# A two-layer decoder on one core: second group of the first attention loaded in the opening stage, one context group fewer loaded ahead, maxima sent by part, two pairs summed by TensorE

## What is computed

```python
x = _layernorm(x + _L0_attn_ref(x, ...))        # 16 heads of 16, 8 masked forward, 8 backward, distance bias
x = _layernorm(x + _L0_xattn_ref(x, ctx, ...))  # 154 context keys, scores clipped at +-10000
x = _layernorm(x + _L0_ffn_ref(x, ...))         # 8 experts, top 2, gelu(x w1) * (x v1)
x = _layernorm(x + _L1_attn_ref(x, ...))        # full attention
x = _layernorm(x + _L1_xattn_ref(x, ctx, ...))  # 154 context keys
x = _layernorm(x + _L1_ffn_ref(x, ...))         # rms norm, causal attention over a latent, rms norm, 8 experts top 2
```

## Time and profile before

| what | value |
|---|---|
| median of 3 runs | 2012.9 us (2011.45 to 2017.55) |
| the profiled execution | 2015.6 us, of which the span is 2013.8 us |
| busy shares | PE 92%, DVE 65%, ACT 48%, POOL 28% |
| mean granted TensorE clock | 0.961 |
| at0, from its first matmul to t1 | about 70.7 to 318 us |
| xa0; xa1 | about 360 to 488; 1362 to 1460 us |
| t3 | about 865 to 949 us |

### The profile page before, as it was taken

One profiled execution on the slowest core, in us unless ns is written; L12 is line 12 of the kernel. 1 busy time (PEld: TensorE's weight loads), 2 busy tenths in 40 slices (PEclk: granted clock), 3 DMA queues, 4 the chain that ended last, 5 costly groups with the idle time before them and its releaser, 6 DMA issues. The chain is left out here.

```text
span 2013.8 us, 34863 instructions
## 1 busy us (share of the span) xinstructions
PE 1857.6 (92%) x12102; PEld 1066.7 (53%) x12103; DVE 1312.1 (65%) x2305; ACT 974.5 (48%) x1906; POOL 562.2 (28%) x939
## 2 busy tenths in 40 slices
PE   8799999888599999989999999987888999987997
PEld 4344445333499999955222222243344444447996
DVE  4588875798733333367988888656787888754113
ACT  3366664566121212244677777743533666632334
POOL 3212223343233333213011111133452111143551
PEclk9899999788799999999999999998998999988999
DMA  7644404410911111055412221055045244051224
GB/s 184 147 93 68 68 4 111 97 34 10 379 55 34 34 34 34 29 166 130 74 33 33 33 42 24 1 128 111 19 101 120 43 64 65 2 209 43 70 70 147
DMA packets 99099, 158.23 MB, mean 79 GB/s; under 512 B 31447, under 2 KB 79063, under 8 KB 93783
## 3 DMA queue, kind: packets, MB, share of 16 engines
q1 hardware_dynamic: 86738, 131.79, 28.7%
q0 software_dynamic: 7488, 20.46, 3.3%
q10 hardware_dynamic: 4736, 4.25, 0.6%
HBM read 110.72 MB, written 44.72 MB: 77 GB/s over the span
## 5 line engine op out<-in xcount | busy, mean ns | idle before, releaser
L2025 ACT ACTIVATE arena<-psum 128x512 f32<-128x512 f32 (+1 forms) x1120 | 575.3, 591 | 285.4 <-PE psum L1981 195.4
L1726 DVE TENSOR_REDUCE arena<-psum 128x1 f32<-128x1024 f32 (+7 forms) x384 | 427.5, 1155 | 71.1 <-PE psum L1684 46.1
L1981 PE MATMUL psum<-arena 99*128 99x512 bf16 (+7 forms) x1280 | 367.4, 353 | 6.9 <-ACT arena L2025 3.9
L1684 PE MATMUL psum<-arena 96*128 96x512 bf16 (+7 forms) x1280 | 348.8, 354 | 19.7 <-DMA arena<-in_alibi_k 9.4
L2557 DVE COPY arena<-arena 128x1536 f32 (+1 forms) x117 | 97.2, 831 | 283.1 <-PE psum L2464 280.5
L1999 PE MATMUL psum<-arena 128*32 128x512 f32 (+3 forms) x2560 | 279.8, 537 | 0.8 <-ACT arena L2025 0.7
L2464 PEld LDWEIGHTS psum<-arena 128*128 128x128 f32 x2340 | 273.1, 191 | 7.1 <-ACT arena L2511 3.1
L2464 PE MATMUL psum<-arena 128*128 128x128 f32 x2340 | 274.1, 275 | 2.2 <-ACT arena L2511 1.4
L1712 DVE CUSTOM_DVE_ANT_0 arena<-psum,arena 128x1024 bf16<-128x1024 f32 (+3 forms) x224 | 217.1, 1018 | 51.6 <-PE psum L1684 51.4
L1981 PEld LDWEIGHTS psum<-arena 99*128 99x128 bf16 (+1 forms) x1280 | 119.6, 99 | 218.9 <-ACT arena L2025 128.5
L1684 PEld LDWEIGHTS psum<-arena 96*128 96x128 bf16 (+1 forms) x1280 | 109.3, 99 | 181.3 <-DVE arena L1726 44.4
(11 more groups left out here) (208 smaller groups left out, 2288.7 us busy)
## 6 DMA issues: line engine op xcount, KB each, us to landing
arena<-k_parts SPq DMA_DIRECT2D x144, 128.0 KB
q_halves<-arena SPq DMA_DIRECT2D x80, 192.0 KB, 2.9
arena<-q_halves SPq DMA_DIRECT2D x40, 384.0 KB, 4.8
arena<-in_L_ffn_up SPq DMA_DIRECT2D x8, 1408.0 KB, 17.5
arena<-q_halves SPq DMA_DIRECT2D x40, 256.0 KB, 5.4
k_parts<-arena SPq DMA_DIRECT2D x48, 192.0 KB, 3.1
arena<-in_L_ffn_down SPq DMA_DIRECT2D x9, 1024.0 KB, 16.2
arena<-y_rows SPq DMA_DIRECT2D x32, 256.0 KB, 4.3
```

Of the source, the lines that this page charges most:

```text
L1684: last = nc.tensor.matmul(dst[:, base + lo:base + hi], q[0:rows, qh, h, qb % 4 * P:qb % 4 * P + P], k[0:rows, h, key0 + lo:key0 + hi], sta ...
L1726: nc.vector.tensor_reduce(dst, src, AX.X, ALU.max).then_inc(t("taken"), 1)
L1981: last = nc.tensor.matmul(b[:, at0:at0 + width], kk[0:rows, h, kb * P:kb * P + P], q[0:rows, qh, h, c0:c1], start=True, stop=diag is None)
L2025: nc.scalar.activation(probs[k % at.ahead][:, heads[0]:heads[-1] + 1, c0:c1], bank[st_bank[no % 3]][:, 0:len(heads) * width].rearrange("p ...
```

## The change

The first attention gets `second_early`: its group 1 goes into the place `stk[2]` and is loaded in t0 by a new SP task "ahead2", which waits until the stores it reads have landed and the context projections are done. Group 2 goes into `stk[1]`. The cross attention loads only group 2 at its start, and then group g + 3 instead of g + 4. The three parts of the maxima are sent one by one, each as soon as GpSimd has written it. In t3, pairs 1 and 3 are summed by TensorE as in t7, with the scaled identities in `floor_t`. The filler after ex0 is 36 turns instead of 55. The planners' numbers follow: `loaded` and `landed` are changed, so that all attention plans and the plans of t0 and t3 are drawn anew.

```diff
+        self.place = (0, 2, 1) if second_early else (0, 1, 2)
...
-        loaded = {0: 0.0, 1: 8.0, 2: 16.0}
+        loaded = {0: 0.0, 1: 0.0, 2: 16.0} if self.second_early else {0: 0.0, 1: 8.0, 2: 16.0}
...
-                landed[j] = queue.split(taken[-1]) + 3.5
+                landed[j] = queue.split(taken[-1]) + 2.5
...
-        loaded = {g: 6.0 * g for g in range(len(self.groups))}
+        loaded = {g: 0.0 if g < 2 else 6.0 if g == 2 else (2 * g - 5) * job_time + 3.0 for g in range(len(self.groups))}
...
-                landed[j] = queue.split(taken[-1]) + 4.0
+                landed[j] = queue.split(taken[-1]) + 3.0
...
-            q, k = stk[g % 3]
+            q, k = stk[at.place[g % 3]]
...
-                    if final and p % 2:
+                    if on_pe(p):
                         task("ACT", "diag", p, 0.9, 0.15)
                         task("PE", "sum", p, 2.6, 0.2, ("diag", p), ("load", p))
                         task("DVE", "moments", p, 1.25, 0.15, ("sum", p))
...
+                    elif following.second_early:
+                        task("SP", "ahead2", 0, 5.0, 8.0, ("ahead", 0), *[("store", v) for v in needed[1]],
+                             *context_ends(layer))
...
+            pe_pairs = (1, 3, 5, 7) if final else (1, 3) if source == "comb" else ()
+
             def on_pe(p):
-                return final and p % 2 == 1
+                return p in pe_pairs
...
                     elif kind == "ahead2":
                         half_stored(sp, 1)
-                        load_queries(sp, following, 1)
+                        if following.keys < S:
+                            load_queries(sp, following, 1)
+                        else:
+                            context.banks_free(sp, layer)
+                            load_group(sp, following, 1)
...
             def diag_of(u, k):
-                at0 = rest_base + 128 * (4 * (u // 4) + 2 * (u % 2) + k)
-                return arena[:, at0:at0 + P]
+                at0 = 128 * (4 * (u // 4) + 2 * (u % 2) + k)
+                if final:
+                    return arena[:, rest_base + at0:rest_base + at0 + P]
+                return floor_t.rearrange("p n q -> p (n q)")[:, at0:at0 + P]
...
+            def part_ready(self, sp, j, n):
+                if n < 2:
+                    sp.wait_ge(self.t("m_step"), 3 * j + (1, 3)[n])
+                else:
+                    sp.wait_ge(self.t("m_parts"), j + 1)
+
             def load(self, sp, j):
                 at, t = self.at, self.t
                 g, qh = at.jobs[j]
-                sp.wait_ge(t("m_parts"), j + 1)
                 for n in range(3):
+                    self.part_ready(sp, j, n)
...
-                load_group(sp, at, 1)
+                if not at.second_early:
+                    load_group(sp, at, 1)
...
                 load_queries(sp, at, 2)
-                load_queries(sp, at, 3)
                 for g in range(ng):
                     maxima.load(sp, 2 * g + 1)
-                    if g + 4 < ng:
-                        load_queries(sp, at, g + 4)
+                    if g + 3 < ng:
+                        load_queries(sp, at, g + 3)
...
-        at0 = SelfAttention("at0", ("fwd", "bwd"), True, q_halves, k_scr)
+        at0 = SelfAttention("at0", ("fwd", "bwd"), True, q_halves, k_scr, second_early=True)
...
-        idle_turns = {"t0": 6, "at0": 1, "t1": 13, "xa0": 1, "rt0": 26, "ex0": 55, "t3": 5, "at1": 1, "t4": 13, "xa1": 1,
+        idle_turns = {"t0": 6, "at0": 1, "t1": 13, "xa0": 1, "rt0": 26, "ex0": 36, "t3": 5, "at1": 1, "t4": 13, "xa1": 1,
```

More of the change, by code:

```diff
@@ L203, with __init__ @@
 class SelfAttention:
-    def __init__(self, name, modes, alibi, q_scr, k_scr, n_early=None):
-        self.name, self.alibi = name, alibi
+    def __init__(self, name, modes, alibi, q_scr, k_scr, n_early=None, second_early=False):
+        self.name, self.alibi, self.second_early = name, alibi, second_early
+        self.place = (0, 2, 1) if second_early else (0, 1, 2)
         self.keys = S
@@ L914, in ring, with nth @@
                 return slice(2 * (p % 4), 2 * (p % 4) + 2)
+            pe_pairs = (1, 3, 5, 7) if final else (1, 3) if source == "comb" else ()
             def on_pe(p):
-                return final and p % 2 == 1
+                return p in pe_pairs
+            def nth(p):
+                return sum(on_pe(n) == on_pe(p) for n in range(p))
             def summed(eng, p):
-                if final:
-                    eng.wait_ge(t("prj_ps" if on_pe(p) else "r"), p // 2 + 1)
-                else:
-                    eng.wait_ge(t("r"), p + 1)
+                eng.wait_ge(t("prj_ps" if on_pe(p) else "r"), nth(p) + 1)
             def row_of(u):
@@ L1177, in diag_of @@
             def diag_of(u, k):
-                at0 = rest_base + 128 * (4 * (u // 4) + 2 * (u % 2) + k)
-                return arena[:, at0:at0 + P]
+                at0 = 128 * (4 * (u // 4) + 2 * (u % 2) + k)
+                if final:
+                    return arena[:, rest_base + at0:rest_base + at0 + P]
+                return floor_t.rearrange("p n q -> p (n q)")[:, at0:at0 + P]
             def pe_sum(pe, p):
-                pe.wait_ge(t("diag"), p // 2 + 1)
+                pe.wait_ge(t("diag"), nth(p) + 1)
                 pe.wait_ge(t(f"rows{p % 4}"), 32 * (p // 4 + 1))
@@ L1309, in dve_add @@
                     if n == 0:
-                        dve.wait_ge(t("first_row"), p + 2 if final else 2 * p + 2)
+                        dve.wait_ge(t("first_row"), 2 * nth(p) + 2)
                 last.then_inc(t("r"), 1)
@@ L1657, in load @@
                 g, qh = at.jobs[j]
-                sp.wait_ge(t("m_parts"), j + 1)
                 for n in range(3):
-                    sp.dma_start(stk[g % 3][0][at.mrow + n:at.mrow + n + 1, qh, :, :]
+                    self.part_ready(sp, j, n)
+                    sp.dma_start(stk[at.place[g % 3]][0][at.mrow + n:at.mrow + n + 1, qh, :, :]
                                  .rearrange("o h (b q) -> o (h b) q", q=P),
@@ L1908, in sp_prog @@
                 for n in (1, 2):
-                    sp.dma_start(stk[n][1][at.mrow:at.mrow + 3, :, :], a["ones"][0:3]).then_inc(t(f"ones{n}"), 16)
-                load_group(sp, at, 1)
+                    sp.dma_start(stk[at.place[n]][1][at.mrow:at.mrow + 3, :, :], a["ones"][0:3]).then_inc(t(f"ones{n}"), 16)
+                if not at.second_early:
+                    load_group(sp, at, 1)
                 if not at.moved_early:
@@ L1968, in pe_scores @@
                 no = at.spans_before[k] + n
-                q, kk = stk[g % 3]
+                q, kk = stk[at.place[g % 3]]
                 rows = at.mrow + 3
```

## The result

The changed kernel takes **1992.2 us** (median of 5 runs, 1983.9 to 1998.7) against 2012.9 before, measured beside it: a ratio of 0.9886 with a 95% interval of 0.9863 to 0.9909. It is faster by 1.1%, and 0.4 us from the 1992.6 us forecast. Two repeats of the same kernel had medians of 1989.3 and 1988.0 us. The profiled execution has a span of 1990.4 us against 2013.8.

A forecast was written before the change was run, and what follows sets the result against it. TensorE was taken to bound most of the kernel, busy 1857.6 of 2013.8 us, VectorE xa0, no engine xa1. Terms -9.4 -2.2 +0.5 -4.5 -1.7 -3.0 = -20.3 took 2015.6 to 1995.3, less 2.7 gives 1992.6 us; range 1982 to 2003.

The forecast's parts named there:

- group 1 early: hole and clock in at0: at0: loading group 1 in t0 removes TensorE's 9.41 us wait (-9.4) and the slow clock behind it (-2.2).
- t0 behind it: t0: SP is busy 5.1 us more and stores go out later, so ScalarE may wait for one; +0.5 us.
- xa1: xa1: fewer query loads and maxima by part remove job 1's 3.31 us wait and shorten others; -4.5, ends 0 and -7.5.
- xa0: xa0: shorter waits for maxima, limited by VectorE being 95% busy; -1.7 us, ends +1 and -4.8.
- t3: t3: TensorE sums pairs 1 and 3, giving an earlier norm and faster first projections; -3.0 us, ends +1.7 and -6.
- plans drawn anew: Whole kernel: the new orders of the plans were counted as 0, with ends 2 us either way.
- The cover that I gave the maxima there, maxima that run 8 us ahead: at0, at1, mla: plans run maxima 8 us ahead, so rows landing 1.23 us earlier bring nothing where TensorE does not wait.
- Rival 5: Cross attentions: scores called too early, TensorE waits 1 us in each of 32 jobs; 2030.8 us, chance 0.06.
- Rival 3: t3: the clock falls before the sums, which cost 4.2 us more, projections stay slow; kernel 1997.3 us, chance 0.08.
- 1: Rival: only the early hole pays, VectorE takes over in the cross attentions, t3 gains nothing; 2001.8 us, chance 0.22.
- 4: Rival: "ahead2" falls behind t0's last stores, so group 1 is issued only some 4 us earlier; 2000.2 us, chance 0.08.
- 2: Rival: everything pays at its upper end, -29.9 us in all; 1983.0 us, chance 0.14.

The follow-up runs named there:

- e9: The kernel before with only the early load of group 1 in t0 added, everything else as before; 2005.3 us, ratio 0.9955.
- e5: The changed kernel with group 1 of at0 loaded in at0 again (`second_early` left out); 1999.5 us, ratio 0.9936.
- e2: The changed kernel with t0 in the order of before, group 1's load put by hand behind the last store it reads; 1988.1 us, ratio 0.9883.
- e11: The changed kernel with t0's order of before, 12 filler turns ahead of t3, and the old planner numbers for xa1 alone; 1984.7 us, ratio 0.9847.
- e3: The changed kernel with the cross attentions' planner given its old numbers, loads and sending as changed; 1991.6 us, ratio 0.9898.
- e10: The changed kernel with everything of the cross attentions as before (plan, maxima sent whole, one query group more ahead); 2000.4 us, ratio 0.9933.
- e7: The changed kernel with pairs 1 and 3 of t3 summed by VectorE again and the filler of 55 turns; 1992.8 us, ratio 0.9894.
- e4: The changed kernel with the three parts of the maxima sent together after the last, in both attention kinds, plans as changed; 1994.3 us, ratio 0.9917.
- e6: The changed kernel with the cross attentions loading one query group more ahead again; 1996.8 us, ratio 0.9925.
- e12: The changed kernel once more, unedited, for the scatter of its stages; 1988.0 us, ratio 0.9870.

## Why the prediction was right, and where it was not

The forecast of 1992.6 us met 1992.2, and the 1995.3 us for the profiled execution met 1992.2 as well. That it is 0.4 us away is luck: the terms were off in both directions and cancelled, the five runs spread over 15 us, and the two repeats came out 3 to 5 us below the forecast. The account is good to a few us and no better:

| step | forecast | stages, before to changed | what else shows it |
|---|---|---|---|
| group 1 early: hole and clock in at0 | -11.6 | -14.0 | e9: -13.0; e5: back by 12.5 |
| t0 behind it | +0.5 (0 to +3) | +4.8 | e9: +4.4; with the old order +1.0 (e2) and +3.0 (e11) |
| xa1 | -4.5 (0 to -7.5) | -2.8 | transfers -7.0 (e3), plan +4.2 |
| xa0 | -1.7 (+1 to -4.8) | -6.5 | none of it in e9, 1.1 in e10, both without the cross part |
| t3 | -3.0 (+1.7 to -6) | -4.2 | e7: first projections end 3.2 later; averages -2.9 |
| plans drawn anew | 0 (2 either way) | in the rows above | t0's wait of 2.1 to 3.5 and the clock behind it; xa1 +4; xa0 not separated from its clock |

*The hole and its clock*: right in place, cause and size. The wait of the earlier trace rows is gone, the clock is 1.00 through all of at0, and e5 brings the wait back with the load. at0 gained 2.4 us more than forecast: 1.4 of them are in e9 too, which sends the parts together, and the last 1.0 us goes with sending by part. The cover that I gave the maxima there, maxima that run 8 us ahead, does not hold everywhere (e4: +1.6).

*What is late next in t0*: the price was +4.8, outside my ends of 0 and +3. The mechanism that I named, the store that ScalarE waits for, is real (7.8 us in e2, 1.0 in the changed kernel) and nearly free (TensorE lost 1.0 us to it in e2). The cost came from the step that I set to nothing, "Plans drawn anew. No row can show this. [...] I take 0". The planner's times for the new task moved the first maxima ahead of projections that had covered group 0's load: 3.0 us of wait and 1.7 us of slower matmuls are nearly all of the 4.8. The earlier trace rows held the warning: the first use at 40.91 us stood without a wait, so it was covered by what is ahead of it, and an order that moves it earlier pays. Together the early load brought 8.3 us (e9) where 11.1 were forecast, and t1 starts 9 us earlier instead of 11.

*One group fewer, by part, in xa1*: the transfers bring 7.0 us, near the upper end of 7.5, and e6 shows the bytes as cause: with four groups ahead the wait of job 1 is 4.1 us. The size came out smaller, 2.8 us, since the new plan costs 4. Job 1's wait, which I had going ("The wait goes"), fell from 3.31 to 1.59 us and is gone only with the old plan (e3). Rival 5 had the mechanism (the plan calls the scores early) and neither the size nor the place: waits for the maxima are 5.5 us in xa1 and 4.3 in xa0, over 32 jobs 0.31 us a job with job 0's in them, under the 0.44 from which it decides and under what stood there before.

*xa0*: mis-sized, beyond its end of -4.8. I read the stage by its 93 us in the middle, where VectorE has 4.6 us of idle time, and by waits of TensorE for the maxima from 362 us on the earlier trace rows, 6.1 us of the 10.2 that the whole stage has. The room was ahead of that middle: VectorE was idle for 12 of the first 35 us, and TensorE ran 20.5 of them at the slow clock. In the changed kernel both are smaller (7 and 6.8 us). That the cross part as a whole brings it is shown (e9, e10). How it divides is not: e3 with the old plan is 3.0 to 5.4 us above the three profiles of the changed kernel, but e2 is 143.0 us with the new one. The number of groups ahead makes none of it (e6). I gave the slow clock no term in xa0, and that is where the executions differ most.

*t3*: right in size. My two reasons, an earlier norm and projections at full clock, are both in e7, which takes back the sums and the filler together; the clock is the larger (2.4 of 3.2 us). The first projection came 0.8 us earlier against its stage, just short of the 1 to 3 that I named. Rival 3 did not come at 36 turns (of nine profiles seven have the clock at 1.00 through t3, and e5 and e12 at 0.50 for 3.4 us, 24 us or more into the stage). At 12 turns its first half came, the fall in the sums, and not its price. The rule of the Trainium skill (TensorE: Matmul & The Clock Gate, "The HAM clock gate"), that the throttled state is the default and only activity releases it, agrees with both: sums at 0.50 behind 6.63 us without work, full clock again within them. That a shorter filler costs time does not follow from it.

*The rivals*: 1 falls with e10 (the cross part pays 10.6 us), 4 with the issues at 47.7 us, and 2 was right for the upper end of xa0 and wrong for t0.

What stays open: how xa0's 6.5 us divide between the plan, the parts and the clock of an execution, how much of e11's 3.3 us is real, whether the old order of t0 is worth anything once at0 is counted with it, and why e7's 3.2 us of t3 show only in part in its median.

## What to carry to other kernels

A fixed order hides loads: before a planner's cost is changed or a task added, list what stands ahead of each first use of a load, and look whether it still does afterwards. A stage bound by one engine is read at its edges too, where that engine starts, and not only by the full stretch in its middle. And a new plan is a part of the change by itself: run the old plan with the new transfers too. Here xa1 was 4 us shorter with the old one. And where the clock of a stage differs between executions of one kernel, as in xa0, one profile of each variant does not tell the variants apart.

## What the runs showed of the hardware

VectorE's busy time in xa0 fell by 4.0 us (122.0 to 118.0) with as many instructions. All of it is the clip of the scores. The groups by line and tile in xa0, before and changed:

```profile
L2169 DVE SCALAR_TENSOR_TENSOR arena<-arena 128x512 f32<-128x512 f32 x80 | 62.6, 798 | 5.0 <-ACT arena L2159 4.8
```

```profile
L2193 DVE SCALAR_TENSOR_TENSOR arena<-arena 128x512 f32<-128x512 f32 x80 | 57.9, 748 | 3.0 <-ACT arena L2183 2.8
```

The length goes with the plan: 786 to 798 ns in the profiles with the old plan (773 in e10), 730 to 759 ns in all with the new one. Most clips take 0.68 us, a few 1.7 and one 2.7. The timeline of the kernel before shows such a long one with two additions of GpSimd inside it:

```profile
418.39 0.78 DVE L1800 TENSOR_REDUCE arena<-psum 128x4 f32<-128x616 f32 x1
419.10 1.73 DVE L2169 SCALAR_TENSOR_TENSOR arena<-arena 128x512 f32<-128x512 f32 x1
```

```profile
419.06 0.63 POOL L1615 TENSOR_TENSOR arena<-arena 128x256 f32<-128x256 f32 x1
419.65 0.63 POOL L1864 TENSOR_TENSOR arena<-arena 128x256 f32<-128x256 f32 x1
```

This is no coincidence. In xa0 of the fourteen profiles 129 clips take over 0.80 us, and every one of them ends 545 to 557 ns after a GpSimd instruction that it overlaps has ended; no clip without a GpSimd instruction beside it takes over 0.70 us. Such a clip behaves as if it stood still until GpSimd is done. It goes the other way too: where GpSimd's addition begins after the clip, the clip keeps its 0.63 us and the addition takes 0.95 instead of 0.63 us, as here, 0.17 us behind the start of a clip at 485.24:

```profile
485.41 0.95 POOL L1864 TENSOR_TENSOR arena<-arena 128x256 f32<-128x256 f32 x1 [1.55 <-DVE arena L1847]
```

What the clips take above 0.68 us adds up to 10.0 us before and 5.8 us in the changed kernel, the whole of the 4 us. Which clips meet GpSimd's additions differs with the plan. The reduction out of PSUM does not show this (778 to 785 ns in all profiles, in both cross attentions).
